# Three in-place additions as accumulating transfers, another product on GpSimd, a new order on four engines, and a placing step laid out in pairs

## The reference

```python
def selective_scan(u, dt, A, Bm, Cm, Dp):
    def step(h, inp):
        u_t, dt_t, B_t, C_t = inp
        dA = jnp.exp(dt_t[:, :, None] * A)
        h = dA * h + (dt_t * u_t)[:, :, None] * B_t[:, None, :]
        y = jnp.einsum('bin,bn->bi', h, C_t)
        return (h, y)
    ...
    return jnp.moveaxis(ys, 0, 1) + u * Dp
...
u = jax.nn.silu(causal_conv(u, cw, cb))
proj = jnp.einsum('bli,ci->blc', u, xp_w)
dt = jax.nn.softplus(jnp.einsum('blr,ir->bli', dt_r, dtw) + dtb)
y = selective_scan(u, dt, A, Bm, Cm, dp) * jax.nn.silu(z)
```

## Time and profile before

| | us |
|---|---|
| median of 3 executions | 14682.76 (14671.36 to 14686.27) |
| the profiled execution | 14673.68 |
| its span, first to last instruction | 14671.9 |
| busy in the span: PE, DVE, ACT, POOL | 12767.7, 13198.2, 11448.7, 13105.2 |

### The profile page before, as it was taken

How to read it: one execution, slowest core, us unless ns; L and a number is a source line. 1 busy time by engine, 2 the same in 40 slices (tenths; PEclk the granted TensorE clock), 3 DMA queues, 4 the chain that set the end, 5 groups by cost and what they waited for, 6 DMA issues and landing times. The chain is left out here.

```text
span 14671.9 us, 199619 instructions
## 1 busy us (share of the span) xinstructions
PE 12767.7 (87%) x51482; PEld 6493.1 (44%) x51482; DVE 13198.2 (90%) x8949; ACT 11448.7 (78%) x21760; POOL 13105.2 (89%) x6096
## 2 busy tenths in 40 slices
PE   7888888888888888888888888888888888888989
PEld 4444444444444444444444444444444444444667
DVE  3999999999999999999999999999999999997323
ACT  4888888888888888888888888888888888886111
POOL 2999999999999999999999999999999999995033
PEclk8998889998889998889998889998889998888799
DMA  3333333333333333333333333333333333332022
GB/s 91 115 123 122 124 119 115 121 118 126 122 120 116 118 120 119 129 115 121 115 123 120 126 118 115 121 117 126 121 123 115 119 118 122 125 118 90 21 64 57
DMA packets 677527, 1660.68 MB, mean 113 GB/s; under 512 B 84687, under 2 KB 331856, under 8 KB 677196
## 3 DMA queue, kind: packets, MB, share of 16 engines
q1 hardware_dynamic: 656712, 1642.87, 33.1%
q0 software_dynamic: 19968, 15.98, 0.7%
q10 hardware_dynamic: 720, 0.55, 0.0%
HBM read 1372.64 MB, written 286.41 MB: 113 GB/s over the span
## 5 line engine op out<-in xcount | busy, mean ns | idle before, releaser
L908 POOL TENSOR_TENSOR dbu<-dtu_rep,b_rep 128x972 f32<-128x972 f32 x4096 | 9122.9, 2255 | 284.6 <-DVE h L842 273.2
L842 DVE TENSOR_TENSOR_SCAN h<-ps,dbu 128x972 f32<-128x972 f32 x4096 | 8856.5, 2173 | 269.7 <-ACT ps L643 260.6
L643 ACT ACTIVATE ps<-dt_rep,A_cur 128x323 f32<-128x323 f32 x12288 | 5842.4, 520 | 323.0 <-DVE h L842 311.1
L851 DVE TENSOR_TENSOR h<-h,ps 128x972 f32<-128x972 f32 x3585 | 4094.4, 1142 | 0.0
L478 PE MATMUL ps<-h,fold 128*32 128x486 f32 x16400 | 3528.4, 719 | 0.4 <-DVE h L851 0.4
L556 PE MATMUL ps<-u_raw,w_cv 128*128 128x162 f32 (+7 forms) x8256 | 1827.0, 374 | 170.1 <-ACT u_raw L679 168.8
L556 PEld LDWEIGHTS ps<-u_raw,w_cv 128*128 128x128 f32 x8256 | 1337.3, 190 | 714.6 <-ACT u_raw L679 299.1
L478 PEld LDWEIGHTS ps<-h,fold 128*32 128x32 f32 x16400 | 714.7, 128 | 1873.5 <-issue 1872.2
L576 PE MATMUL ps<-u_act,w_x 128*128 128x324 f32 x1548 | 855.8, 723 | 516.6 <-ACT u_act L694 509.7
L465 PE MATMUL ps<-c_rows,sel_c 16*128 16x324 f32 x2048 | 827.1, 483 | 375.0 <-DVE h L851 374.9
L916 POOL TENSOR_TENSOR h<-h,c_rep 128x972 f32<-128x972 f32 x513 | 1150.3, 2242 | 0.0
(11 more groups left out here) (189 smaller groups left out, 14184.1 us busy)
## 6 DMA issues: line engine op xcount, KB each, us to landing
dt_rep<-dt_rows SPq DMA_DIRECT2D x1028, 486.0 KB, 4.6
dtu_rep<-dtu_rows SPq DMA_DIRECT2D x1028, 486.0 KB, 4.9
b_rep<-b_rows SPq DMA_DIRECT2D x1028, 162.0 KB, 4.8
dt_rows<-dt SPq DMA_DIRECT2D x257, 486.0 KB, 2.7
dtu_rows<-dtu SPq DMA_DIRECT2D x257, 486.0 KB, 3.0
c_rep<-b_rows SPq DMA_DIRECT2D x513, 162.0 KB, 3.6
w_cv<-in_w_cv SPq DMA_DIRECT2D x17, 768.0 KB, 7.1
b_rows<-xp_rows SPq DMA_DIRECT2D x258, 40.5 KB, 4.7
```

The costliest lines, as they stand in the source:

```text
L643: ins = act.activation(decay[s % 2][:, it * L + 1:(it + 1) * L], dt_rep[:, s % NR, it, 1:L], ACT.Exp, scale=A_cur[:, it * N + s:it * N + s ...
L842: dve.tensor_tensor_scan(h[s % RING][:, :, :].rearrange("p i t -> p (i t)"), decay[s % 2], dbu[s % DRING][:, :, :].rearrange("p i t -> p ( ...
L851: dve.tensor_tensor(h[s % RING][:, :, :], h[s % RING][:, :, :], c_ps.unsqueeze(1).broadcast_to([128, IT, L]), ALU.mult).then_inc(s_prod, 1)
L908: pool.tensor_tensor(dbu[s % DRING][:, :, :], dtu_rep[:, r, :, :], b_rep[:, q, :].unsqueeze(1).broadcast_to([128, IT, L]), ALU.mult).then_ ...
```

## The change

Four things are changed.

1. Steps 0 to 2 of `ge_dt` are no longer tensor additions on GpSimd but transfers from SBUF to SBUF with an add (`accum_op`), issued from GpSimd's queue. Each waits until the one before has landed (`s_acc`), and step 3 and SP's store of `dt` wait for the third. The correction is now added with its sign turned, so that all three are additions. Their order is `exp_x`, `dtu`, `u_pre`.
2. `ON_POOL` goes from (4, 12) to (3, 7, 12): GpSimd makes three products a unit, VectorE 13 instead of 14.
3. The hand-written orders of all five engines change; VectorE's products stand further behind their scans.
4. In `place_tokens` the one-hot tiles are laid out so that the elements of one product lie 2 elements apart, in pairs; the stationary and the moving operand change places, the result comes out already turned, and `put` is made by five instructions instead of one.

```diff
-ON_POOL = (4, 12)
+ON_POOL = (3, 7, 12)
...
         def ge_dt(pool, p, par, step):
 
-            if step == 0:
-                reached(pool, s_sp, 4 * p + 1)
-                pool.tensor_tensor(dt[:, :], dt[:, :], exp_x[:, :], ALU.add).then_inc(s_dt, 1)
-            elif step == 1:
-                reached(pool, s_dt, 4 * p + 1)
-                reached(pool, s_sp, 4 * p + 4)
-                pool.tensor_tensor(dt[:, :], dt[:, :], u_pre[:, :], ALU.subtract).then_inc(s_dt, 1)
-            elif step == 2:
-                reached(pool, s_dt, 4 * p + 2)
-                pool.tensor_tensor(dt[:, :], dt[:, :], dtu[:, :], ALU.add).then_inc(s_dt, 1)
+            if step < 3:
+                term, ready, at = ((exp_x, 1, 0), (u_pre, 4, 2), (dtu, 2, 1))[step]
+                reached(pool, s_sp, 4 * p + ready)
+                wait(pool, s_acc, 16 * (3 * p + at))
+                pool.sem_inc(s_held, 1)
+                pool.dma_start(dt[:, :], term[:, :], accum_op=ALU.add).then_inc(s_acc, 16)
             else:
-                reached(pool, s_dt, 4 * p + 3)
+                wait(pool, s_acc, 16 * (3 * p + 3))
                 reached(pool, s_ua, p + 1)
...
         def vector_step(dve, u, par, scan=True, a1=True, b1=True):
...
-                ve_scan(dve, u, 9)
-                ve_product(dve, u, 8)
-                ve_scan(dve, u, 10)
-                ve_product(dve, u, 9)
-                ve_scan(dve, u, 11)
-                ve_product(dve, u, 10)
-                ve_scan(dve, u, 12)
-                ve_product(dve, u, 11)
+                ve_scan(dve, u, 9)
+                ve_scan(dve, u, 10)
+                ve_scan(dve, u, 11)
+                ve_product(dve, u, 8)
+                ve_product(dve, u, 9)
+                ve_product(dve, u, 10)
+                ve_product(dve, u, 11)
+                ve_scan(dve, u, 12)
...
-                    dve.tensor_tensor(put[e % NH][:, :, :, :], at_hi[:, e, :, :].unsqueeze(2).broadcast_to([TS, SL, 5, TPC * CH]),
-                                      vals[:, e, :, :].unsqueeze(1).broadcast_to([TS, SL, 5, TPC * CH]), ALU.mult).then_inc(s_lo, 1)
+                    for v in range(5):
+                        ins = dve.tensor_tensor(put[e % NH][:, :, :, v, :],
+                                                at_hi[:, e, :, :].rearrange("p h (j k) -> p j h k", k=2),
+                                                vals[:, e, v, :].rearrange("p (j k) -> p j k", k=2).unsqueeze(2)
+                                                .broadcast_to([TS, J2, SL, 2]), ALU.mult)
+                    ins.then_inc(s_lo, 1)
...
-                        mm = pe.matmul(ps[0:5 * SL, e % 2, 0:TS], put[e % NH][:, :, :, :].rearrange("p h v j -> p (h v) j")[:, :, j],
-                                       at_lo[e % NH][:, :, j], start=(j == 0), stop=(j == TPC * CH - 1))
+                        mm = pe.matmul(ps[0:TS, 0, e * 5 * SL:(e + 1) * 5 * SL], at_lo[e % NH][:, j // 2, :, j % 2],
+                                       put[e % NH][:, j // 2, :, :, j % 2].rearrange("p h v -> p (h v)"),
+                                       start=(j == 0), stop=(j == TPC * CH - 1))
```

More of the change, by code:

```diff
@@ L622, in tensor_step @@
                 te_sum(pe, u, 2)
+            if a1:
+                te_xp(pe, k, par)
+            if scan:
                 te_sum(pe, u, 3)
             if a1:
-                te_xp(pe, k, par)
                 te_dt(pe, k, 0)
@@ L684, in se_conv @@
                 reached(act, s_ua, k)
-                reached(act, s_dt, 4 * k - 2)
+                wait(act, s_acc, 48 * k)
             act.copy(half_of(u_pre, half), pj).then_inc(s_cvev, 1)
@@ L750, in se_softplus @@
             elif step == 2:
-                reached(act, s_dt, 4 * p - 2)
+                wait(act, s_acc, 48 * p)
                 reached(act, s_ua, p + 1)
@@ L768, in scalar_step @@
                 se_copy_A(act, u)
+                se_decay(act, u, 0)
+                se_decay(act, u, 1)
             if b1:
                 se_softplus(act, p, 0)
[L771 to L773 removed]
             act.preload_act_table_set(LOG_SET)
@@ L955, in gpsimd_step @@
             if scan:
+                ge_dbu(pool, u, 4)
+                ge_dbu(pool, u, 5)
                 ge_dbu(pool, u, 6)
                 ge_dbu(pool, u, 7)
+            if b1:
+                ge_dt(pool, p, 1 - par, 2)
+            if scan:
+                ge_product(pool, u, 3)
                 ge_dbu(pool, u, 8)
@@ L1006, in sp_store_dt @@
         def sp_store_dt(sp, p, which):
-            reached(sp, s_dt, 4 * p + 3 + which)
+            if which:
+                reached(sp, s_dtu, p + 1)
+            else:
+                wait(sp, s_acc, 16 * (3 * p + 3))
             sp.sem_inc(s_go, 1)
@@ L1031, in sync_step @@
             p = u + 1
+            if scan:
+                sp_load_c(sp, u, par, 2)
             if b1:
+                sp_load_b(sp, u, par, 0)
                 sp_store_dt(sp, p, 0)
@@ L1722, in _, with place_tokens @@
                     chore(k)
-def place_tokens(nc, cst, keep, index, weight):
+def place_tokens(nc, keep, index, weight):
     lo, vals, at_hi, iota = keep["lo"], keep["vals"], keep["at_hi"], keep["iota"]
@@ L1733, in sem @@
             return ctx.enter_context(nc.semaphore(name))
-        at_lo = [sb(f"p_lo{i}", [TS, TS, TPC * CH], BF16) for i in range(NH)]
-        put = [sb(f"p_put{i}", [TS, SL, 5, TPC * CH], BF16) for i in range(NH)]
-        turned = [sb(f"p_turned{i}", [5 * SL, TS]) for i in range(2)]
+        at_lo = [sb(f"p_lo{i}", [TS, J2, TS, 2], BF16) for i in range(NH)]
+        put = [sb(f"p_put{i}", [TS, J2, SL, 5, 2], BF16) for i in range(NH)]
         lists = sb("p_lists", [TS, E_N * SL, 5])
@@ L2026, in program @@
             shared_and_choice(nc, cst, x_T, nrm, ins, n_rows, out, keep)
-            place_tokens(nc, cst, keep, index, weight)
+            place_tokens(nc, keep, index, weight)
         experts(nc, cst, ins, n_rows, index, weight, out)
```

111 lines of the change are left out of this document (46 added, 65 removed).

## The result

The changed kernel takes 14538.42 us (median of 4, 14534.74 to 14540.76), the kernel before 14684.51 (median of 4): ratio 0.9902, interval 0.9885 to 0.9919, 146 us less where 503 were forecast. The profiled execution took 14539.11 us.

The account below looks back on a forecast made before the run. VectorE was taken to bound the layers before, GpSimd 1.1 us behind, and GpSimd after; TensorE the placing. 14673.7 - 381 (layers) - 122 (placing) = 14171, median 9 above: 14180 us, range 13940 to 14620.

Parts of the forecast that it names:

- TensorE too. Their waits ... cost 0: Layers: ScalarE and TensorE keep their instructions; their waits on GpSimd's products of s = 3 and 7 cost 0.
- so I count that stall as gone: VectorE's gate: it comes 3.2 us later, so its 0.9 us wait for TensorE's sums disappears.
- The decays' part of the stalls: VectorE in a unit: waits on ScalarE's decays, about 0.5 us, stay before the scan of s = 15.
- The rest of the layers' forecast: Layers: GpSimd becomes the bound, a unit takes 49.7 us, 1.49 less, 381 us over 256 units.
- the first rival: Layers: VectorE stays the bound if an issue costs 1.0 us or less; unit 48.8 us, kernel 13950 us; 27%.
- x, the price of an issue: GpSimd in a unit: each of three transfer issues costs 1.30 us, bounds 0.99 and 1.92, or 2.3 by rows.
- Landing: Transfers in a unit: each lands 5.5 us after issue, just hidden against limits of 5.7 and 7.2 us.
- The dear issues: GpSimd's issues cost as much as the scatter's, 1.92 us: unit 51.6 us, kernel 14660 us; 14%.
- the late landing: Transfers land too late and GpSimd stands; slower from 7.4 us on, 15840 us at 9.7; 8%.
- VectorE blocking the issues: Issues wait for VectorE's running instruction: 3.1 us more a unit, kernel 14970 us; within the late landing's 8%.
- Ring between GpSimd and VectorE: Layers, `dbu` and scans: the ring takes 48.9 us, under GpSimd's own 49.5, so it adds nothing.
- Placing: `place_tokens`: an expert takes 5.8 us instead of 13.44, TensorE at 120 ns a product, saving 122 us.

Follow-up runs that it names:

- e5: Changed kernel plus nine zero-adding TensorE products of 128 columns in its gap before the broadcast of C, order kept: 14208 us, ratio to before 0.9682.
- e3: Changed kernel with TensorE's sum of tiles 12 and 13 ahead of the broadcast of C again: 14332 us, ratio to before 0.9763.
- e7: Changed kernel with VectorE's product of s = 2 on 648 of its 972 elements, a third left out: 14204 us, ratio to before 0.9680.
- e8: Changed kernel with one more VectorE instruction of 324 elements ahead of the product of s = 2: 14287 us, ratio to before 0.9736.
- e1: Kernel before with part 4 alone, the placing in pairs: 14538.88 us, ratio to before 0.9904.
- e9: Kernel before with one more VectorE instruction of 324 elements ahead of the product of s = 2: 14732 us, ratio to before 1.0006.
- e10: Kernel before with VectorE's product of s = 2 on 648 of its 972 elements, the rest left out: 14722 us, ratio to before 0.9998.
- e11: Kernel before with part 1 alone, three accumulating transfers in place of GpSimd's additions: 14730 us, ratio to before 0.9999.
- e2: Changed kernel with VectorE's product of s = 2 on 3 of its 972 elements, the rest left out: 14207 us, ratio to before 0.9678.
- e12: Changed kernel with the sum ahead of the broadcast, three zero-adding products before that sum and five before the x projection: 14234 us, ratio to before 0.9666.
- e13: Kernel before with 4, 8 and 3 zero-adding products ahead of the first sum, x projection and second half of step sizes: 14790 us, ratio 1.0073.
- e14: Changed kernel with the nine zero-adding products of e5 placed behind the sum of s = 2 and 3 instead: 14640 us, ratio to before 0.9974.

## Why the prediction was wrong, point by point

- *The step that failed* is "TensorE too. Their waits ... cost 0", with "so I count that stall as gone": a unit was taken as the longest of separate lists, GpSimd's or VectorE's. TensorE's new order, a part of the diff, was given no price. It put the broadcast ahead of the sum; TensorE idled 2.6 us, its clock fell, and three of its steps took 7.56 us instead of 4.54 (e5's same three). The stall of the gate grew from 0.90 to 1.07 us, those on decays from about 1.05 to 1.7, and the 1.1 us taken off VectorE were given back. e3 and e5 show it from two sides: 0.9 and 1.3 us a unit, by the ratios 0.0139 and 0.0220 of 14684, 204 and 323 us. The order alone doesn't cost this much: e7 and e8 keep it, and the stall is gone in those units in which the low stretch falls elsewhere. It is the order together with a low stretch at the same place of every unit. The decays' part of the stalls, 1.6 us a unit where the prediction counted 0.5, was mis-sized on its own account: 1.3 us of it are left in e5. (For the kernel before, VectorE's list and its idle times, 49.4 + 0.90 + 1.05, give 51.35, so these sums are good to about 0.2 us.)
- *The rest of the layers' forecast* then comes out: 49.7 us forecast, 49.87 in e5. But not by its reason. GpSimd was never the bound there (scans wait 22.0 us in all for `dbu` in e5); VectorE's 48.3 plus 1.4 us of waits was. That is the first rival, whose unit of 48.8 was too low since it had only 0.5 us of decay waits. Two errors offset each other; that this figure comes out is luck.
- *x, the price of an issue*: taken 1.30, bounds 0.99 to 1.92; measured 0.61 to the next start. Taking the record of a gather, 0.99, as the lower bound was the error: a record can run beside the next instruction, so the pitch is what counts.
- *Landing*: taken 5.5, measured 4.4, 4.5 and 5.3; hidden, as said, against limits of 5.7 and 7.2. Of the two estimates from the Trainium skill in the prediction, 4.3 by Collectives: The Full Stack is near the 4.4 and 4.5 and too low for the 5.3, and 3.1 by DMA: Bandwidth & Descriptors is too low; the measurement decides.
- *The dear issues, the late landing, VectorE blocking the issues*: none is seen.
- *Ring between GpSimd and VectorE*: adds nothing, as said.
- *Placing*: forecast -122, measured -140 (e1). An expert takes 4.67 us instead of 5.8: TensorE keeps up with 13752.10 - 13747.43 = 4.67 us of VectorE, 97 ns a product (taken 120). VectorE is the bound there, at 4.67 instead of 3.9, as the five `put` take 13752.10 - 13750.19 = 1.91 us, 0.38 each (taken 0.22). Either the fixed part of a small instruction was read too low from two large ones, or the new layout of `put` is slower for an element; no run tells them apart.

**What stays open.** Why both kernels stand at 51.19 us. Six kernels do on average (before, changed, e1, e9, e10, e11, each 51.19 to 51.21), with work on VectorE and GpSimd that differs by over 1 us. In four of them (before, changed, and nearly all units of e1 and e11) the units are alike and the stretches at 0.50 keep their place; in e9 and e10 neither holds, and the average is the same. In e2, e3, e5, e7, e8 and e12, at 49.8 to 50.3, the stretches move about. That a steady low stretch and a steady unit hold each other in place (a shorter unit would meet the clock elsewhere) fits the four, but is argued, not shown, and e9 and e10 need more than that. Nor does the share of the low clock settle it: executions of the kernel before on the occasion of e13 and e14 had mean granted clocks from 0.895 to 0.926, and all took between 14674.07 and 14682.93 us. e13, meant to test the account on the kernel before, is inconclusive. Nor was the 0.9 us wait for the skip products, left in e5 and e12, taken away.

## What to carry to other kernels

When work is taken off the two busiest engines of a kernel whose engines all idle a little, follow one unit around its ring, through every engine whose order the change touches, and price each wait that is moved; "needed only later" must be checked against the engine that waits next. A wait of TensorE ahead of a run of products can be paid twice, once as idle time and once in the clock behind it, as here in every unit of the changed kernel and in some units of e8: order its list so that ready work stands ahead of the wait, or fill the gap, and read the granted clock there in more than one unit. And a time that doesn't answer to small changes of work in either direction isn't set by the work of that engine alone; a third of an instruction more or less is a cheap test.

## What the runs showed of the hardware that was not expected

- More work made a kernel faster, twice: 324 elements more on VectorE (e8, 51.19 to 50.22 us a unit) and nine products on zeros (e5, to 49.87); the same nine elsewhere gave 51.54. In both it is the low stretches behind the turn of the unit that became fewer: the broadcast's products take 507 and 483 ns on average against 568.
- The accumulating transfer of 486 KB inside SBUF cost GpSimd 0.6 us until its next start and landed in 4.4 to 5.3 us. GpSimd's tensor instructions have longer records in that kernel (`dbu` 2529 ns against 2255 on average), right behind an issue and well away from one, but still start 7020.75 - 7018.55 = 2.20 us apart: a longer mean was no longer pitch.
- Of bf16 operands whose neighbours lie 4 bytes apart, with 30 columns moving, a product came every 97 ns at 1.2 GHz, VectorE setting the pace (window below, granted clock 0.50); at 96 bytes and 108 columns it was 277 ns. Whether it was the spacing or the columns, no run tells apart.

```profile
13745.00:13827.00 82.00, 74.47 (x768) 72.82 (x768) 75.68 (x99) 0.83 (x2) 0.00 (x0) 0.50 0.01 1
```
